# A two-layer decoder on one core: the softmax peak of two of four score banks applied by ScalarE's bias instead of a VectorE subtraction

## The chip, the core and the metric

The kernel runs on one core of a Trainium2 chip. The core's engines run side by side and meet only at semaphores: TensorE (PE; its weight loads are PEld), VectorE (DVE), ScalarE (ACT), GpSimd (POOL) and SyncE (SP, which here only issues DMAs). Each engine takes its own instructions strictly in program order. PSUM, into which TensorE writes, has eight banks of 128 partitions by 512 f32; SBUF is the working memory. The metric is the device time of one launch in microseconds (us), where less is better.

## What is computed

Two decoder layers on x of 16 x 128 x 256 (16 sequences, here called tiles, of 128 tokens). Every step is a sublayer, a residual sum and a layer norm:

```python
x = _layernorm(x + _L0_attn_ref(...))     # l0: latent attention with rotary embedding, 16 heads
x = _layernorm(x + _L0_xattn_ref(ctx, x)) # x0: linear attention
x = _layernorm(x + _L0_ffn_ref(...))      # f0: gated FFN, fp4 levels
x = _layernorm(x + _L1_attn_ref(...))     # l1: causal attention plus a second branch (ma)
x = _layernorm(x + _L1_xattn_ref(x, ctx)) # x1: cross attention and a ReLU FFN
x = _layernorm(x + _L1_ffn_ref(...))      # f1: one linear layer, fp6 levels
```

Three of these have a softmax over 128 keys, for 16 heads of each tile: l0, l1 and x1, thus 48 softmaxes of 128 x (16 heads x 128 keys). With the scale s, what is computed is exp(s * score - s * peak), with peak the largest score of a row and head; the sum of a row is taken along with the values and divided out later.

## The kernel before

**Staging.** Each tile goes through 55 stages (`STAGES`), and four tiles are under way at a time. `TIMELINE` is a table of numbers: it gives each stage of each tile a slot, with a tile 122 slots after the one before, and every engine writes its instructions for the stages in the order of these slots. No scheduler reorders anything: an instruction that waits holds back all that stands behind it on its engine. In the middle of the run the same pattern returns once per tile, with stages of four tiles laced into each other. Per tile it has one `l0_scores`, one `x1_scores` and one `l1_scores`, and in the pattern they come in this order; x1 and l1 stand close together.

**Banks.** Banks 0 to 3 (`s0` to `s3`) hold scores; banks 4 to 7 go round in a ring among all other results of TensorE. Two semaphores of a bank, full and empty, count its fills and its emptyings. `free` makes TensorE wait until the bank's last content has been read, `emptied` marks the instruction that has read it.

**A softmax.** TensorE writes the scores of 16 heads, 4 per bank, with the mask summed in. The banks are handled in the order `BANK_ORDER = (2, 3, 0, 1)`:

- VectorE (`softmax`, L912 to L939) takes the peak of 4 heads of a bank in one reduction (L918). For banks 2 and 3 it then writes the peak times -s to `low` (L925, 128 x 4). For banks 0 and 1 it subtracts the peak from the scores, 128 x 512, from PSUM into `prob` (L929), which also frees the score bank.
- ScalarE (`exps`, L649 to L666) takes exp of banks 2 and 3 head by head: 8 instructions of 128 x 128 that read PSUM, with a column of `low` as bias (L663). For banks 0 and 1 it takes exp of 128 x 512 at once, in place in `prob`, without a bias (L657).
- TensorE (`mix`, L1299 to L1309) turns `prob` over, 4 transposes per bank into a bank of the ring (recorded at L1240), ScalarE copies each into `probT` (recorded at L601), and TensorE weighs the values with it.

**What stands around it.** Helpers record much of the work under one line: all matmuls under L1125, transposes of tiles under L1240, copies by ScalarE under L601. Behind the exps of x1 on ScalarE stand the copy of the turned f1 input (L601), two biased reads of l1's queries (L712) and two tanh (L717), of which the last frees the bank that TensorE's third turn of x1's `prob` needs. Behind the exps of l1 stands the copy of the turned x of x0 (`xt_`, L601), which TensorE needs for `x0_project`. Behind the exps of l0 stand two copies of the turned FFN hidden (`scratch`, L601), each of which frees a ring bank, and then the first copy to `probT`, which frees a third; the matmuls of `f0_down` (with `w_dn`) need all three.

Of the kernel before, what the change touches and what calls it, by code (L numbers as in the profile page):

```python
# [14 lines left out]
P = 128  # L15
TILES, D, HEADS, HD, LAT = 16, 256, 16, 16, 32
FFN, HID = 704, 1024
KD = D // P
GROUP = 4
# [5 lines left out]
ALU = mybir.AluOpType  # L25
ACT = mybir.ActivationFunctionType
# [10 lines left out]
SCALES = {"l0": LAT ** -0.5, "l1": HD ** -0.5, "x1": HD ** -0.5}  # L37
# [38 lines left out]
S_BANKS = ["s0", "s1", "s2", "s3"]  # L76


BANK_ORDER = (2, 3, 0, 1)
# [19 lines left out]
SCORES = ["l0_scores", "l1_scores", "x1_scores"]  # L99
# [46 lines left out]
def of_turn(i, b, value):  # L146


    if isinstance(i, int):
        return value(i * GROUP + b)  # L150
    reg, off = i
    found = [value((turn + off) * GROUP + b) for turn in range(1, ITERS)]
    step = found[1] - found[0]
    assert all(found[n] == found[0] + n * step for n in range(len(found))), (b, found)
    return reg * step + (found[0] - step)


def at(i, stages, stage, b, n=1, j=0):


    seq = [(s, t) for _, s, t in TIMELINE if s in stages]
    return of_turn(i, b, lambda t: seq.index((stage, t)) * n + j + 1)


def decoder_kernel(nc, x, xT, ctxT, mask, cols, rows, const, bconst, c_attn, blocks, wqk, cproj,
                   x0_w, gate_up, down, l1_w, x1_w, w1, w2, fw, out):
    with ExitStack() as ctx:
        def sb(name, shape, dt=F32):
            return ctx.enter_context(nc.sbuf_tensor(name, shape, dt))

        def sem(name):
            return ctx.enter_context(nc.semaphore(name))

        bank = [ctx.enter_context(nc.psum_tensor(f"bank{k}", [P, 512], F32)) for k in range(8)]
# [65 lines left out]
        prob = sb("prob", [P, 4, 512])  # L240
# [1 line left out]
        ma_ = sb("ma_", [P, 4, 512])  # L242

        peak = sb("peak", [P, GROUP, HEADS])
        low = sb("low", [P, GROUP, 8])
        inv_sum = sb("inv_sum", [P, GROUP, HEADS])
        stats = sb("stats", [P, GROUP, 6])
        mean_var = sb("mean_var", [P, GROUP, 2])
# [35 lines left out]
        def long(ap, n):  # L284

            return ap.unsqueeze(2).broadcast_to([ap.shape[0], ap.shape[1], n])

        def rows4(ap):
            return ap.rearrange("p (c t) -> p c t", c=4)
# [35 lines left out]
        x_biased = sem("x_biased")  # L325
        q_swap, q_cos, q_sin, q_done = sem("q_swap"), sem("q_cos"), sem("q_sin"), sem("q_done")
        k_cos, k_swap, k_done = sem("k_cos"), sem("k_swap"), sem("k_done")
        peaked, lowered, exped, inverse = sem("peaked"), sem("lowered"), sem("exped"), sem("inverse")
        parted, varied, eps_in, rooted = sem("parted"), sem("varied"), sem("eps_in"), sem("rooted")
        x_new, affine = sem("x_new"), sem("affine")  # L330
        scaling, quant, dequant = sem("scaling"), sem("quant"), sem("dequant")
# [3 lines left out]
        def count(i, key):  # L335

            if i is None:
                return WHERE[key][0], WHERE[key][1] + 1
            stage, b, name = key
            return WHERE[stage, b, name][0], of_turn(i, b, lambda t: WHERE[stage, t, name][1] + 1)  # L340

        def wait_full(eng, i, key):

            k, value = count(i, key)
            eng.wait_ge(full[k], value)
            return bank[k]

        def wait_empty(eng, i, key):

            k, value = count(i, key)  # L350
            eng.wait_ge(empty[k], value)
# [7 lines left out]
        def emptied(ins, key):  # L359
            ins.then_inc(empty[WHERE[key][0]], 1)  # L360
# [236 lines left out]
        def _(act):  # L597
# [51 lines left out]
            def exps(layer):  # L649

                stage = layer + "_scores"

                def f(i, b):
                    for r in BANK_ORDER:
                        if r < 2:
                            wait_empty(act, i, (stage, b, S_BANKS[r]))
                            act.activation(prob[:, r, :], prob[:, r, :], ACT.Exp, scale=SCALES[layer])\  # L657
                                .then_inc(exped, 1)
                            continue
                        act.wait_ge(lowered, at(i, SCORES, stage, b, 2, r - 2))  # L660
                        for c in range(4):
                            h = 4 * (r - 2) + c
                            ins = act.activation(prob[:, r, c * P:(c + 1) * P], bank[r][:, c * P:(c + 1) * P],  # L663
                                                 ACT.Exp, scale=SCALES[layer], bias=low[:, b, h:h + 1])
                        emptied(ins, (stage, b, S_BANKS[r]))
                return f  # L666
# [93 lines left out]
        def _(dve):  # L760
# [10 lines left out]
            src = wait_full(dve, None, "p_g")  # L771
# [4 lines left out]
            src = wait_full(dve, None, "p_latb")  # L776
# [135 lines left out]
            def softmax(layer):  # L912

                stage = layer + "_scores"

                def top(i, b, r):
                    src = wait_full(dve, i, (stage, b, S_BANKS[r]))
                    dve.tensor_reduce(peak[:, b, 4 * r:4 * r + 4], rows4(src[:, :]), AX_X, ALU.max)\  # L918
                        .then_inc(peaked, 1)

                def take(i, b, r, n):
                    dve.wait_ge(peaked, at(i, SCORES, stage, b, 4, n))
                    if r >= 2:

                        dve.tensor_scalar(low[:, b, 4 * r - 8:4 * r - 4], peak[:, b, 4 * r:4 * r + 4],  # L925
                                          -SCALES[layer], None, ALU.mult).then_inc(lowered, 1)
                        return
                    src = bank[r]
                    emptied(dve.tensor_tensor(rows4(prob[:, r, :]), rows4(src[:, :]),  # L929
                                              long(peak[:, b, 4 * r:4 * r + 4], P), ALU.subtract),  # L930
                            (stage, b, S_BANKS[r]))

                def f(i, b):
                    for n, r in enumerate(BANK_ORDER):
                        top(i, b, r)
                        if n:
                            take(i, b, BANK_ORDER[n - 1], n - 1)
                    take(i, b, BANK_ORDER[3], 3)
                return f  # L939
# [167 lines left out]
        def _(pe):  # L1107
# [129 lines left out]
            def turn_tile(i, key, src, n=KD, moved=()):  # L1237
                dst = free(i, key, moved)
                for k in range(n):
                    ins = pe.transpose(dst[:, k * P:(k + 1) * P], src[:, k * P:(k + 1) * P], ident)  # L1240
                filled(ins, key)
# [57 lines left out]
            def mix(layer):  # L1299

                def f(i, b):
                    for r in BANK_ORDER:
                        key = (layer + "_mix", b, f"t{r}")
                        if r < 2:
                            pe.wait_ge(exped, at(i, SCORES, layer + "_scores", b, 2, r))
                        else:
                            wait_empty(pe, i, (layer + "_scores", b, S_BANKS[r]))
                        turn_tile(i, key, prob[:, r, :], 4)
                return f  # L1309

# [267 lines left out]
```

## Time and profile before

| | |
|---|---|
| median of 3 runs | 1174.74 us (1174.51 to 1176.31) |
| the profiled execution, its own time | 1172.23 us |
| its span, first to last instruction | 1170.4 us |
| mean granted clock of TensorE | 0.936 of full |
| PE busy | 946.8 us, 81% |
| DVE busy | 888.7 us, 76% |
| ACT busy | 509.1 us, 43% |
| POOL busy | 309.4 us, 26% |
| the chain that ended last | DVE 47%, PE 30%, ACT 11%, issue 6%, POOL 6% |

Shares of busy time say how much an engine does, not whether the end waits for it. The chain that ended last is followed back from the last instruction, at each step to what released it; its shares say where the end is set. The pattern of one tile takes about 65 us, and it is in its rows, in order of time, that one sees which engine is last at which point.

### The profile page before, as it was taken

How to read it: one execution, taken by the hardware profiler on the slowest of the kernel's cores; microseconds unless marked ns; L12 is line 12 of the kernel's file. 1: busy time of each engine (PE TensorE's matmuls, PEld its weight loads, DVE VectorE, ACT ScalarE, POOL GpSimd, SP SyncE). 2: the span in 40 equal slices, each digit the busy share in tenths (PEclk: the TensorE clock that was granted, in tenths of full speed). 3: DMA queues.
4: the chain of work that ended last, by engine and by line, in shares of the span. 5: the costliest groups of instructions: out<-in, count | busy, mean ns of one | idle time of the engine just before them, and what ended most of it. 6: DMA issues, size and time to landing. Idle time of an engine off the chain costs nothing.

```text
span 1170.4 us, 23205 instructions
## 1 busy us (share of the span) xinstructions
PE 946.8 (81%) x8774; PEld 752.5 (64%) x8774; DVE 888.7 (76%) x2135; ACT 509.1 (43%) x1377; POOL 309.4 (26%) x508
## 2 busy tenths in 40 slices
PE   5657778888888888888888888888888888878754
PEld 5444656676676776776767766767666767657633
DVE  3775677888797888788797888878887888777452
ACT  2322436363536355363636354453636263534320
POOL 2561121312222222223222232232222222312121
PEclk9677999999999999999999999999999999989876
DMA  9102000000000000000000000000000000000000
GB/s 338 37 5 73 10 8 15 3 19 8 20 8 15 10 17 10 14 14 3 20 7 15 13 15 11 16 11 3 24 3 20 3 6 8 6 6 6 6 4 5
DMA packets 24414, 24.47 MB, mean 21 GB/s; under 512 B 2305, under 2 KB 22641, under 8 KB 24177
## 3 DMA queue, kind: packets, MB, share of 16 engines
q1 hardware_dynamic: 24304, 22.98, 6.1%
q8 instruction: 72, 1.18, 0.4%
q14 instruction: 38, 0.30, 0.1%
HBM read 18.80 MB, written 2.10 MB: 18 GB/s over the span
## 4 chain that ended last, share of the span: by engine, by line
DVE 47%; PE 30%; ACT 11%; issue 6%; POOL 6%; DMA 0%; DVEq 0%; POOLq 0%; SPq 0%
PE bank L1125 21%; PE bank L1240 9%; DVE peak L918 7%; ACT prob L663 6%; ACT prob L657 3%; DVE ma_ L1037 3%; DVE stats L847 2%; DVE q_top L809 2%; DVE y_ L861 2%; POOL scratch L528 2%; POOL rstd L522 2%; DVE k_ L1061 2%; DVE scratch L905 2%; DVE x_ L873 1%; DVE k_ L1070 1%
## 5 line engine op out<-in xcount | busy, mean ns | idle before, releaser
L663 ACT ACTIVATE prob<-bank,low 128x128 f32<-128x128 f32 x384 | 104.4, 382 | 156.6 <-DVE low L925 156.6
L1240 PE MATMUL bank<-cst,prob 128*128 128x128 f32 x768 | 117.2, 303 | 54.7 <-DVE y_ L861 39.0
L519 POOL TENSOR_TENSOR var_eps<-mean_var,rsq 128x1 f32<-128x1 f32 x144 | 28.4, 198 | 468.3 <-DVE mean_var L850 468.3
L1240 PEld LDWEIGHTS bank<-cst,prob 128*128 128x128 f32 x768 | 96.1, 156 | 71.9 <-issue 62.6
L918 DVE TENSOR_REDUCE peak<-bank 128x4 f32<-128x512 f32 x192 | 126.3, 684 | 20.8 <-PE bank L1125 20.8
L601 ACT ACTIVATE xt_<-bank 128x256 f32<-128x256 f32 x144 | 54.9, 393 | 130.5 <-PE bank L1240 130.3
L601 ACT ACTIVATE probT<-bank 128x512 f32<-128x512 f32 x192 | 103.5, 602 | 17.4 <-PE bank L1240 17.4
L522 POOL TENSOR_TENSOR rstd<-var_eps,rsq 128x1 f32<-128x1 f32 x144 | 79.8, 554 | 11.3
L1125 PE MATMUL bank<-w_gu,xt_ 128*128 128x352 f32 x256 | 81.0, 470 | 1.5 <-ACT w_f L601 1.0
L1125 PE MATMUL bank<-xt_,w 128*128 128x128 f32 x512 | 70.5, 304 | 0.5 <-ACT xt_ L601 0.5
L1125 PEld LDWEIGHTS bank<-xt_,w 128*128 128x128 f32 x512 | 69.4, 221 | 1.2 <-ACT xt_ L601 1.2
L1125 PEld LDWEIGHTS bank<-w_gu,xt_ 128*128 128x128 f32 x256 | 49.9, 196 | 27.6 <-issue 3.2
L847 DVE BATCH_NORM_STATS2 stats<-y_ 128x6 f32<-128x256 f32 x144 | 61.5, 427 | 5.0
L1240 PE MATMUL bank<-cst,y_ 128*128 128x128 f32 x128 | 27.8, 300 | 45.7 <-DVE y_ L886 34.1
L563 POOL TENSOR_TENSOR scratch<-scratch,q_scale 128x704 f32<-128x704 f32 x16 | 22.2, 1385 | 156.7 <-DVE scratch L822 156.7
L1125 PE MATMUL bank<-k_,q_ 32*128 32x128 f32 (+2 forms) x1040 | 61.3, 347 | 0.0
L929 DVE TENSOR_TENSOR prob<-bank,peak 128x512 f32<-128x512 f32 x96 | 61.3, 679 | 0.0
L509 POOL TENSOR_TENSOR xb_<-x_,rowt 128x256 f32<-128x256 f32 x80 | 60.0, 757 | 2.7 <-DVE x_ L873 2.7
L657 ACT ACTIVATE prob<-prob 128x512 f32<-128x512 f32 x96 | 57.4, 676 | 0.0
L563 POOL TENSOR_TENSOR k_<-q_,q_scale 128x256 f32<-128x256 f32 x32 | 19.8, 617 | 137.4 <-DVE q_ L822 137.4
L1240 PE MATMUL bank<-cst,k_ 128*128 128x128 f32 x64 | 15.0, 319 | 50.5 <-POOL k_ L563 50.5
L638 ACT ACTIVATE scratch<-bank,lat_bias 128x128 f32<-128x128 f32 x128 | 36.5, 367 | 43.8 <-PE bank L1125 43.8
(180 smaller groups left out, 2202.7 us busy)
## 6 DMA issues: line engine op xcount, KB each, us to landing
xtin<-in_xT SPq DMA_DIRECT2D x16, 128.0 KB, 2.3
next_<-in_x SPq DMA_DIRECT2D x16, 128.0 KB, 6.9
ct_<-in_ctxT SPq DMA_DIRECT2D x16, 128.0 KB, 7.7
w<-in_w SPq DMA_DIRECT2D x2, 1024.0 KB, 6.1
out<-x_ SPq DMA_DIRECT2D x16, 128.0 KB, 1.7
next_<-x_ SPq DMA_DIRECT2D x16, 127.0 KB
rowt<-in_rows SPq DMA_DIRECT2D x1, 1664.0 KB, 7.7
w<-in_gate_up SPq DMA_DIRECT2D x2, 512.0 KB, 9.4
```

Of the source, the lines that this page charges most:

```text
L509: pool.tensor_tensor(xb_[:, b, :], source(b), term, ALU.add).then_inc(x_biased, 1)
L522: pool.tensor_tensor(rstd[:, b:b + 1], var_eps[:, b:b + 1], rsq[:, 1:2], ALU.pow)\
L563: pool.tensor_tensor(to(b).rearrange("p (a k) -> p a k", k=block), lev(b).rearrange("p (a k) -> p a k", k=block), long(q_scale[:, b % 2, a ...
L601: emptied(act.activation(dst, src, ACT.Copy), key)
L638: ins = act.activation(dst[:, c * P:(c + 1) * P], src[:, c * P:(c + 1) * P], ACT.Identity, bias=lat_bias[:, off + c:off + c + 1])
L657: act.activation(prob[:, r, :], prob[:, r, :], ACT.Exp, scale=SCALES[layer])\
L663: ins = act.activation(prob[:, r, c * P:(c + 1) * P], bank[r][:, c * P:(c + 1) * P], ACT.Exp, scale=SCALES[layer], bias=low[:, b, h:h + 1])
L847: dve.bn_stats(stats[:, b, :], y_[:, b, :]).then_inc(parted, 1)
L918: dve.tensor_reduce(peak[:, b, 4 * r:4 * r + 4], rows4(src[:, :]), AX_X, ALU.max)\
L929: emptied(dve.tensor_tensor(rows4(prob[:, r, :]), rows4(src[:, :]), long(peak[:, b, 4 * r:4 * r + 4], P), ALU.subtract), (stage, b, S_BANK ...
L1125: return pe.matmul(dst, lhsT, rhs, start=first, stop=last, **more)
L1240: ins = pe.transpose(dst[:, k * P:(k + 1) * P], src[:, k * P:(k + 1) * P], ident)
```

## The change

For banks 0 and 1, VectorE now does what it did for banks 2 and 3: it writes the peak times -s to `low`, and no longer subtracts. ScalarE takes exp of these banks too head by head from PSUM, with `low` as bias. `low` grows from 8 to 16 columns. Banks 0 and 1 are now freed by the fourth exp of each and no longer by the subtraction, and TensorE's turns wait for that instead of for the semaphore `exped`, which is gone. Per softmax 2 subtractions of 128 x 512 and 2 exps of 128 x 512 go; 2 products of 128 x 4 and 8 exps of 128 x 128 come.

```diff
-        low = sb("low", [P, GROUP, 8])
+        low = sb("low", [P, GROUP, HEADS])
...
-                    for r in BANK_ORDER:
-                        if r < 2:
-                            wait_empty(act, i, (stage, b, S_BANKS[r]))
-                            act.activation(prob[:, r, :], prob[:, r, :], ACT.Exp, scale=SCALES[layer])\
-                                .then_inc(exped, 1)
-                            continue
-                        act.wait_ge(lowered, at(i, SCORES, stage, b, 2, r - 2))
+                    for n, r in enumerate(BANK_ORDER):
+                        act.wait_ge(lowered, at(i, SCORES, stage, b, 4, n))
                         for c in range(4):
-                            h = 4 * (r - 2) + c
+                            h = 4 * r + c
                             ins = act.activation(prob[:, r, c * P:(c + 1) * P], bank[r][:, c * P:(c + 1) * P],
                                                  ACT.Exp, scale=SCALES[layer], bias=low[:, b, h:h + 1])
                         emptied(ins, (stage, b, S_BANKS[r]))
...
                     dve.wait_ge(peaked, at(i, SCORES, stage, b, 4, n))
-                    if r >= 2:
-
-                        dve.tensor_scalar(low[:, b, 4 * r - 8:4 * r - 4], peak[:, b, 4 * r:4 * r + 4],
-                                          -SCALES[layer], None, ALU.mult).then_inc(lowered, 1)
-                        return
-                    src = bank[r]
-                    emptied(dve.tensor_tensor(rows4(prob[:, r, :]), rows4(src[:, :]),
-                                              long(peak[:, b, 4 * r:4 * r + 4], P), ALU.subtract),
-                            (stage, b, S_BANKS[r]))
+                    dve.tensor_scalar(low[:, b, 4 * r:4 * r + 4], peak[:, b, 4 * r:4 * r + 4],
+                                      -SCALES[layer], None, ALU.mult).then_inc(lowered, 1)
...
-                        if r < 2:
-                            pe.wait_ge(exped, at(i, SCORES, layer + "_scores", b, 2, r))
-                        else:
-                            wait_empty(pe, i, (layer + "_scores", b, S_BANKS[r]))
+                        wait_empty(pe, i, (layer + "_scores", b, S_BANKS[r]))
```

No other instruction changes its place. On ScalarE, from the exps of x1 to what follows the exps of l1, there stood:

```order
L663 ACTIVATE prob<-bank,low 128x128 x8
L657 ACTIVATE prob<-prob 128x512 x2
L601 ACTIVATE xt_<-bank 128x256
L712 ACTIVATE q_<-bank,colt 128x128 x2
L717 ACTIVATE xt_<-bank,k_bias 128x128 x2
L723 ACTIVATE ka_<-xt_,colt 128x256 x2
L601 ACTIVATE probT<-bank 128x512 x4
L663 ACTIVATE prob<-bank,low 128x128 x8
L657 ACTIVATE prob<-prob 128x512 x2
L601 ACTIVATE xt_<-bank 128x256
L601 ACTIVATE yt_<-bank 128x512
```

and after the exps of x1 there now stands, to the same point (L658 is the exp of every bank, L707, L712 and L718 are L712, L717 and L723 of before):

```order
L707 ACTIVATE q_<-bank,colt 128x128 x2
L712 ACTIVATE xt_<-bank,k_bias 128x128 x2
L718 ACTIVATE ka_<-xt_,colt 128x256 x2
L601 ACTIVATE probT<-bank 128x512 x4
L658 ACTIVATE prob<-bank,low 128x128 x16
L601 ACTIVATE xt_<-bank 128x256
L601 ACTIVATE yt_<-bank 128x512
```

Where 8 narrow and 2 wide exps stood there are 16 narrow ones, and the same copies stand behind them.

## Rows read from the trace of the kernel before

**Rows 1.** The page: PE's and others' busy time; the chain by engine and line.

```profile
PE 946.8 (81%) x8774; PEld 752.5 (64%) x8774; DVE 888.7 (76%) x2135; ACT 509.1 (43%) x1377; POOL 309.4 (26%) x508
...
DVE 47%; PE 30%; ACT 11%; issue 6%; POOL 6%; DMA 0%; DVEq 0%; POOLq 0%; SPq 0%
PE bank L1125 21%; PE bank L1240 9%; DVE peak L918 7%; ACT prob L663 6%; ACT prob L657 3%; DVE ma_ L1037 3%; DVE stats L847 2%; DVE q_top L809 2%; DVE y_ L861 2%; POOL scratch L528 2%; POOL rstd L522 2%; DVE k_ L1061 2%; DVE scratch L905 2%; DVE x_ L873 1%; DVE k_ L1070 1%
```

**Rows 2.** Groups of the softmax: count | busy us, mean ns | idle before.

```profile
L663 ACT ACTIVATE prob<-bank,low 128x128 f32<-128x128 f32 x384 | 104.4, 382 | 156.6 <-DVE low L925 156.6
...
L929 DVE TENSOR_TENSOR prob<-bank,peak 128x512 f32<-128x512 f32 x96 | 61.3, 679 | 0.0
...
L657 ACT ACTIVATE prob<-prob 128x512 f32<-128x512 f32 x96 | 57.4, 676 | 0.0
...
L925 DVE TENSOR_SCALAR low<-peak 128x4 f32<-128x4 f32 x96 | 22.0, 229 | 0.0
```

**Rows 3.** The chain in order of time, x1 then l1: start us, us, what.

```profile
565.86 1.04 ACT prob L657 x2
...
567.68 0.53 ACT xt_ L717 x2
...
574.52 1.04 ACT prob L657 x2
...
575.88 1.60 PE bank L1125 x12
```

**Rows 4.** Timeline at x1's exps: start us, us, engine, line, what [idle before <-releaser].

```profile
563.68 2.17 ACT L663 ACTIVATE prob<-bank,low 128x128 f32<-128x128 f32 x8 [3.25 <-DVE low L925]
565.70 1.20 ACT L657 ACTIVATE prob<-prob 128x512 f32<-128x512 f32 x2
566.73 0.43 ACT L601 ACTIVATE xt_<-bank 128x256 f32<-128x256 f32 x1
...
568.34 1.06 PE L1240 MATMUL bank<-cst,prob 128*128 128x128 f32 x8 [0.40 <-ACT xt_ L717]
```

**Rows 5.** Timeline at l1's exps, DVE, then PE.

```profile
573.49 1.28 DVE L929 TENSOR_TENSOR prob<-bank,peak 128x512 f32<-128x512 f32 x2
574.69 0.68 DVE L967 TENSOR_TENSOR scratch<-bank,rowt 128x512 f32<-128x512 f32 x1
...
575.88 1.16 PE L1125 MATMUL bank<-xt_,w_x 128*128 128x128 f32 x8 [1.08 <-ACT xt_ L601]
```

**Rows 6.** Timeline at l0's exps of a tile with full clock: ACT, then PE.

```profile
678.76 0.92 ACT L601 ACTIVATE scratch<-bank 128x512 f32<-128x512 f32 x2
679.50 0.66 ACT L601 ACTIVATE probT<-bank 128x512 f32<-128x512 f32 x1
...
681.08 2.95 PE L1125 MATMUL bank<-w_dn,scratch 128*128 128x256 f32 x12
```

**Rows 7.** Timeline at l0's exps of an earlier tile: PE.

```profile
547.37 0.63 PE L1240 MATMUL bank<-cst,prob 128*128 128x128 f32 x4 [1.82 <-DVE y_ L861]
548.50 2.79 PE L1240 MATMUL bank<-cst,prob 128*128 128x128 f32 x12 [0.51 <-DVE y_ L861]
```

**Rows 8.** Busy time by stretch, one tile's pattern each; PEclk is the granted clock.

```profile
546.48:611.34 64.86, 55.91 (x542) 44.79 (x542) 53.09 (x131) 31.21 (x86) 17.15 (x30) 0.97 0.04 12
...
870.71:937.05 66.34, 57.64 (x542) 46.42 (x542) 53.26 (x131) 31.20 (x86) 17.16 (x30) 0.95 0.04 10
937.05:1000.25 63.20, 54.24 (x542) 43.25 (x542) 53.08 (x131) 31.00 (x86) 17.11 (x30) 1.00 0.02 7
```

**Rows 9.** The same view, four short stretches at half clock.

```profile
275.43:278.85 3.42, 3.42 (x19) 3.42 (x17) 3.14 (x7) 0.69 (x1) 0.00 (x0) 0.50 0.00 0
548.50:551.92 3.42, 3.42 (x14) 3.26 (x15) 1.76 (x5) 2.21 (x4) 1.92 (x4) 0.50 0.00 0
664.55:667.97 3.42, 3.42 (x18) 3.42 (x17) 3.14 (x7) 0.69 (x1) 0.00 (x0) 0.50 0.00 0
1002.47:1005.89 3.42, 3.42 (x15) 3.23 (x14) 1.72 (x6) 2.02 (x4) 1.72 (x4) 0.50 0.00 0
```

More of the change, by code:

```diff
@@ L327, in decoder_kernel @@
         k_cos, k_swap, k_done = sem("k_cos"), sem("k_swap"), sem("k_done")
-        peaked, lowered, exped, inverse = sem("peaked"), sem("lowered"), sem("exped"), sem("inverse")
+        peaked, lowered, inverse = sem("peaked"), sem("lowered"), sem("inverse")
         parted, varied, eps_in, rooted = sem("parted"), sem("varied"), sem("eps_in"), sem("rooted")
```

## Prediction, made from the kernel before alone

> **What bounds the kernel now.** I read the page first, then the chain in order of time, then the timeline where the chain touches a softmax, then the granted clock by stretch.
>
> The page makes VectorE look like the engine to relieve: it is 76% busy, with 47% of the chain, and ScalarE is 43% busy with 11% of it [rows 1]. But the chain by line names the exps too: L663 has 6% and L657 has 3%, while L929, the subtraction that the change takes away, is not among the lines shown [rows 1]. 3% of 1170.4 us is about 34 us, and a pair of the wide exps takes 1.04 us on the chain [rows 3]; 34 / 1.04 is about 32 pairs. There are 48 softmaxes, 16 each of l0, x1 and l1. So two of three softmaxes have their exps on the path.
>
> The chain in order of time says which [rows 3]. At x1 it runs through the wide exps, the tanh of l1_project (L717) and then TensorE's turns; at l1 it runs through the wide exps and straight on to a matmul. The timeline gives the reason. At x1, 8 turns on TensorE waited 0.40 us for ScalarE's L717, which had to free a ring bank [rows 4]. At l1, the matmuls of x0_project waited 1.08 us for the copy of xt_, which stands behind the exps on ScalarE [rows 5]. At l0 it is otherwise: TensorE waits for VectorE's residual sum (L861) twice, 1.82 and 0.51 us [rows 7].
>
> TensorE's clock is the second matter. Three tiles' patterns have the same number of instructions and take 63.20 us at clock 1.00, 64.86 at 0.97 and 66.34 at 0.95 [rows 8]. The difference is stretches at half clock (1.2 GHz instead of 2.4), none, one or two of them per pattern. Rows 9 has four: 12 of them begin between 275 and 1003 us (the first and the last row are the first and the last of these), about one per tile. The one at l0's turns (548.50) comes after TensorE had idled 1.82 us and shortly after that 0.51 us [rows 7]; the other (664.55) comes after a gap in which TensorE waits for VectorE's affine norm of x1. One of them costs 64.86 - 63.20 = 1.66 us, and two cost 3.14.
>
> **The change part by part.**
>
> *ScalarE, each softmax.* 8 narrow exps pace at 565.70 - 563.68 = 2.02 us, 0.253 each. The two wide ones pace at 566.73 - 565.70 = 1.03 us [rows 4]. The change puts 8 more narrow ones where the two wide ones stood: + 2.02 - 1.03 = + 0.99 us until the next instruction on ScalarE starts. The added exps are of the very form of L663 (128 x 128 from PSUM, a column of `low`), so the row is the price itself; bounds are the smallest step between two (0.25) and the full 0.382 us that one takes alone [rows 2], which would give + 1.0 to + 2.0 us; I take 0.253, since they are issued back to back.
>
> The Trainium skill has another price. Its page "ScalarE: Activation LUTs" (What ACT_TABLE_LOAD costs) puts an ACTIVATE with a pointer bias at about 280 ns plus 0.833 ns per column, one with immediates at 186 ns plus the same, with 93 ns of overlap. As an estimate from that page 8 narrow exps would take 2.35 us and the two wide ones 1.04 us, + 1.31 per softmax. The wide pair agrees with the trace's 1.03 us and the narrow ones are quicker in the trace (2.02), so the measurement decides; by the page the sum below would be 10 us higher. The page also speaks against the change in principle: the fixed part is paid once per instruction.
>
> *VectorE, each softmax.* Two subtractions go, which pace at 574.69 - 573.49 = 1.20 us [rows 5]. Two products to `low` come; those there are average 0.229 us [rows 2], but part of each lies under the reduction beside it, and the last of the four has to wait for its own peak as the last subtraction did. I put the saving at 0.9 us (bounds 0.7 and 1.1), 43 us over 48 softmaxes. What of it reaches the end is the question, not its size.
>
> *x1, 16 times.* All four `low` are written before ScalarE gets to bank 0, so ScalarE runs through 16 exps and reaches the copy, L712 and L717 0.99 us later. TensorE's turns of bank 0 already waited 0.40 us for L717, so there is no slack: the wait grows to about 1.4 us, l1's scores come 0.99 later, and with them VectorE's next peaks. VectorE has its 0.9 us in hand, but it waits there for TensorE. 16 x 0.99 = 15.8 us.
>
> *l1, 16 times.* The copy of xt_ comes 0.99 us later, and TensorE already waited 1.08 us for it. VectorE is idle after this until x0's results come, so its saving is again spent in waiting. 16 x 0.99 = 15.8 us.
>
> *l0, 16 times.* Here VectorE's residual sum comes 0.9 us earlier and TensorE could begin its turns earlier. But the third and fourth turns need ring banks that ScalarE frees by the two copies to `scratch`, and f0_down needs the bank that the first copy to `probT` frees; these three stand behind the exps. Before, with full clock, that copy began at 679.50 and took 0.66, so it ended at 680.16, and f0_down began at 681.08 [rows 6]. The three copies move back by 0.99: the copy ends at 681.15, and f0_down can begin at about 681.2. ScalarE's loss eats VectorE's gain to within 0.1 us: + 0.1 x 16 = + 1.6 us. The bounds are - 0.3 (where the turns run at half clock, ScalarE's copies had more slack) and + 0.3, so - 5 to + 5 us.
>
> *Bank release.* Score banks 0 and 1 are freed about 2 us later than before. The next scores are written over 3 us after the turns that need the same exps, in TensorE's own order, so nobody waits: 0. The product to `low` queues nothing new, and `exped` costs nothing to drop. SP and GpSimd are untouched.
>
> *TensorE's clock.* The added 0.99 us at l1 makes one gap of about 2.1 us where there was one of 1.08, and at x1 about 1.4 where there was 0.40. The gap of 1.82 us at l0 is cut in two, but the one before the third turn grows. Gaps of this size are what stood before half-clock stretches so far [rows 7, 9]. So the pattern now has one more place at which a stretch can follow, at l1, where TensorE is on the path right after. Bounds: none of today's 12 stretches left (- 20 us), to one more in each of the 13 patterns in full swing (+ 21 us). I take an extra one in every other pattern: 6 x 1.66 = + 10 us, because one place goes weaker (l0) and one is new.
>
> **The sum.** The profiled execution took 1172.2 us, its span plus 1.8. 1172.2 + 15.8 + 15.8 + 1.6 + 10 = 1215.4 us. The median of the runs lies 2.5 us above the profiled execution, so 1218 us.
>
> **Rivals.**
>
> *The exps cost what they cost and the clock does as before.* 1174.7 + 31.6 + 1.6 = 1208 us. For it: today's number of stretches hardly varies from tile to tile. Against: longer gaps on TensorE.
>
> *The new rhythm spares the stretches.* Patterns without any exist today, 63.20 us [rows 8], and a different length of the pattern may miss them all: 1208 - 20 = 1188 us. In between lie 1190 to 1205.
>
> *More stretches or dearer exps.* One more stretch in each pattern, 1208 + 21 = 1229 us; or exps nearer to 0.29 us each, 10 us more, 1228 with the forecast's clock.
>
> *Faster.* VectorE with its 47% of the chain decides, at l0: if TensorE's f0_down doesn't need to wait for ScalarE's copies, the 0.9 us comes through 16 times, and if in x1 and l1 the copies behind the exps were hidden, nothing would be lost: 1174.7 - 14 = 1160 us. It decides only if both waits on ScalarE in rows 4 and 5 are misread, that is, if TensorE would have been held there by something else for another 0.99 us. The rows name ScalarE with 0.40 and 1.08 us of plain idle time, and the chain passes there. For no change at all the l0 gain would have to come through in double.
>
> That the change doesn't do what it says can be left out: the built kernel has 16 narrow exps per softmax on ScalarE and no subtraction on VectorE.
>
> **How the numbers follow.** Forecast with about half an extra stretch per pattern (1210 to 1224): 0.45. Clock as before (1204 to 1210): 0.22. Fewer stretches (1188 to 1204): 0.12. More stretches or dearer exps (1224 to 1238): 0.17. Faster: 0.03. No change: 0.01. Range 1198 to 1230: it leaves out half of the cases with fewer stretches, a third of those with more, and the rivals below. A measurement of this kernel can tell about 0.2% (2.3 us) from no change; slower by more than that has 0.96, faster 0.03, within it 0.01.
>
> **What would show it.** On the page: ACT's busy time up by some 45 us and its share of the chain up from 11% to 14 or 15%, DVE's busy time down by 45 to 55. In the timeline at l1: the wait of x0_project for the copy of xt_ at about 2.1 us, and at x1 the turns' wait for the tanh at about 1.4. At l0: TensorE's wait before the third turn naming ScalarE's copy to scratch instead of VectorE's sum. A pattern with full clock takes about 65.2 us, and those with stretches 66.9 and 68.5. The prediction is wrong if that pattern stays at 63.2 (then the path isn't through these exps), or if the number of half-clock stretches is far from 18.

## The result, and the profile after

The changed kernel takes 1270.01 us (median of 4 runs, 1268.87 to 1274.74), beside 1175.53 us for the kernel before in the same job: 1.081 times as long, 95% interval 1.078 to 1.0841. The forecast was 1218, with a range up to 1230. Slower was right; the loss is 95 us where 43 were forecast.

From the page of the changed kernel, the lines that answer [rows 1] (busy time, the chain by engine and by line), and the groups that answer [rows 2] (count | busy us, mean ns | idle before):

```profile
span 1267.1 us, 23493 instructions
PE 1002.9 (79%) x8774; PEld 793.8 (63%) x8774; DVE 837.1 (66%) x2135; ACT 558.0 (44%) x1665; POOL 307.0 (24%) x508
...
DVE 38%; PE 33%; ACT 19%; POOL 5%; issue 4%; DMA 0%; DVEq 0%; POOLq 0%; SPq 0%
PE bank L1113 23%; ACT prob L658 16%; PE bank L1228 10%; DVE peak L913 5%; DVE ma_ L1025 2%; DVE stats L842 2%; POOL scratch L528 2%; POOL rstd L522 2%; DVE q_top L804 2%; DVE k_ L1049 1%; DVE scratch L900 1%; DVE x_ L868 1%; DVE k_ L1058 1%; DVE y_ L881 1%; DVE y_ L878 1%
...
L658 ACT ACTIVATE prob<-bank,low 128x128 f32<-128x128 f32 x768 | 203.5, 413 | 173.4 <-DVE low L918 173.4
```

```profile
L918 DVE TENSOR_SCALAR low<-peak 128x4 f32<-128x4 f32 x192 | 36.9, 204 | 0.1
```

The work moved as meant. VectorE is busy 51.6 us less (888.7 to 837.1), ScalarE 48.9 us more (509.1 to 558.0). TensorE has the same 8774 matmuls, yet is busy 56.1 us more (946.8 to 1002.9). That is the first sign of a slower clock. ScalarE has 19% of the chain, where the prediction looked for 14 or 15%. The 16% of L658 are about 203 us, which is 48 times the 4.23 us that 16 exps take; so now all three softmaxes have their exps on the chain, l0's too.

The same view of stretches as in [rows 8], of three patterns of the changed kernel, from one start of l0's exps to the next (us, then busy us with counts of PE, PEld, DVE, ACT, POOL, then PEclk):

```profile
660.49:732.22 71.73, 60.58 (x544) 48.17 (x543) 49.79 (x131) 34.17 (x103) 16.95 (x30) 0.90 0.04 12
732.22:803.86 71.64, 60.47 (x544) 48.16 (x543) 49.71 (x131) 34.17 (x104) 16.97 (x30) 0.90 0.04 11
874.48:943.19 68.71, 57.18 (x542) 45.83 (x542) 49.79 (x131) 34.13 (x103) 16.96 (x30) 0.95 0.04 12
```

A pattern takes 71.7 us where it took 63.2 to 66.3 [rows 8], at a clock of 0.90. The next rows, of the same view, are the stretches at half clock within one pattern and the first of the next one; they answer [rows 9]:

```profile
647.98:651.39 3.41, 3.37 (x10) 2.23 (x11) 3.20 (x7) 1.07 (x2) 0.73 (x1) 0.50 0.02 5
665.04:668.45 3.41, 3.09 (x12) 2.85 (x13) 1.58 (x4) 2.61 (x6) 1.34 (x4) 0.50 0.00 0
685.52:688.93 3.41, 3.30 (x32) 2.49 (x36) 0.75 (x2) 3.02 (x6) 0.00 (x0) 0.50 0.02 5
695.76:699.17 3.41, 3.41 (x16) 3.41 (x17) 0.55 (x2) 0.99 (x3) 0.10 (x1) 0.50 0.00 0
719.66:723.07 3.41, 3.28 (x10) 2.14 (x11) 3.23 (x8) 1.07 (x2) 0.73 (x1) 0.50 0.00 0
```

There are four per pattern: at the turn of x1's hidden, at l0's turns, at x1's turns and behind l1's exps. The kernel before had one per pattern, taking one with another. Counted by the granted clock in the traces, over twelve patterns in the middle of the run (222.0 to 998.2 us before, 230.3 to 1087.1 us after), it had 11, and the changed kernel has 45. The fifth row is the first one again, 71.68 us later. The pattern returns with its stretches in the same places, tile after tile: from 217.90 to 839.12 us every pattern has its four. One pattern that has only two of them (874.48) takes 3.0 us less than its neighbours, 1.5 for each.

The gaps that TensorE has in these places, from the timeline of the changed kernel (start us, us, engine, line, what [idle before <-releaser]); the first two rows are l0, then come x1 and l1, then the turn of the hidden:

```profile
663.54 0.63 PE L1228 MATMUL bank<-cst,prob 128*128 128x128 f32 x4 [0.50 <-DVE y_ L856]
665.36 1.94 PE L1228 MATMUL bank<-cst,prob 128*128 128x128 f32 x8 [1.20 <-ACT scratch L601]
...
684.60 0.63 PE L1228 MATMUL bank<-cst,prob 128*128 128x128 f32 x4 [1.66 <-ACT xt_ L601]
...
685.63 1.94 PE L1228 MATMUL bank<-cst,prob 128*128 128x128 f32 x8 [0.40 <-ACT xt_ L712]
...
695.69 2.04 PE L1113 MATMUL bank<-xt_,w_x 128*128 128x128 f32 x8 [2.11 <-ACT xt_ L601]
...
648.02 0.69 PE L1228 MATMUL bank<-cst,y_ 128*128 128x128 f32 x2 [2.21 <-DVE y_ L881]
```

The gap ahead of the turn of the hidden is no longer than it was in the kernel before, where it also stood in patterns that had no stretch behind it, as here:

```profile
598.25 0.44 PE L1240 MATMUL bank<-cst,y_ 128*128 128x128 f32 x2 [2.21 <-DVE y_ L886]
```

### The profile page after: what moved, and what is told of

Its sections match the earlier page's. It is cut to its first block, busy times and chain, and to the rows that moved or that the text cites. A ratio compares the mean times of both kernels' runs of the same rounds, so it can differ in the third digit from the quotient of the medians.

```text
span 1267.1 us, 23493 instructions
## 1 busy us (share of the span) xinstructions
PE 1002.9 (79%) x8774; PEld 793.8 (63%) x8774; DVE 837.1 (66%) x2135; ACT 558.0 (44%) x1665; POOL 307.0 (24%) x508
## 4 chain that ended last, share of the span: by engine, by line
DVE 38%; PE 33%; ACT 19%; POOL 5%; issue 4%; DMA 0%; DVEq 0%; POOLq 0%; SPq 0%
PE bank L1113 23%; ACT prob L658 16%; PE bank L1228 10%; DVE peak L913 5%; DVE ma_ L1025 2%; DVE stats L842 2%; POOL scratch L528 2%; POOL rstd L522 2%; DVE q_top L804 2%; DVE k_ L1049 1%; DVE scratch L900 1%; DVE x_ L868 1%; DVE k_ L1058 1%; DVE y_ L881 1%; DVE y_ L878 1%
## 5 line engine op out<-in xcount | busy, mean ns | idle before, releaser
L658 ACT ACTIVATE prob<-bank,low 128x128 f32<-128x128 f32 x768 | 203.5, 413 | 173.4 <-DVE low L918 173.4
L1228 PE MATMUL bank<-cst,prob 128*128 128x128 f32 x768 | 138.8, 336 | 78.6 <-ACT xt_ L601 24.1
L1228 PEld LDWEIGHTS bank<-cst,prob 128*128 128x128 f32 x768 | 113.9, 177 | 97.1 <-issue 72.5
L1113 PE MATMUL bank<-xt_,w_x 128*128 128x128 f32 x256 | 46.8, 342 | 34.4 <-ACT xt_ L601 34.4
L856 DVE TENSOR_TENSOR y_<-bank,x_ 128x256 f32<-128x256 f32 x32 | 13.6, 425 | 80.6 <-PE bank L1113 80.6
L1113 PEld LDWEIGHTS bank<-xt_,w_x 128*128 128x128 f32 x256 | 41.5, 245 | 40.1 <-ACT xt_ L601 38.9
L1113 PE MATMUL bank<-k_,q_ 32*128 32x128 f32 (+2 forms) x1040 | 66.2, 366 | 0.0
L1113 PE MATMUL bank<-xt_,w 128*128 128x128 f32 x512 | 64.8, 288 | 0.5 <-ACT xt_ L601 0.5
L1113 PEld LDWEIGHTS bank<-k_,q_ 32*128 32x128 f32 (+1 forms) x1040 | 49.8, 209 | 13.4 <-issue 10.0
L1113 PE MATMUL bank<-w_dn,scratch 128*128 128x256 f32 x192 | 56.0, 442 | 0.8 <-ACT scratch L601 0.8
```

The costliest lines, as they stand in the source:

```text
L1113: return pe.matmul(dst, lhsT, rhs, start=first, stop=last, **more)
```

## The experiments

Two theories. **A, the clock:** of the 6.8 us that a pattern gained (64.86 to 71.7), some 2 are ScalarE's longer exps on the path, and the rest is half clock behind TensorE's longer gaps. **B, the price:** the exps themselves cost over 3 us at x1 and at l1, and the clock only goes along. All runs of one job share their runs of the kernel before (1173.6 to 1175.3 us).

### TensorE kept busy in its gaps

In both kernels TensorE gets fillers, matmuls whose result is overwritten unread. The diff is that of the changed kernel, 35 fillers per tile. The kernel before has other gaps and gets 7 ahead of l0's first turn and 2 behind it, 1 behind x1's second turn, 4 ahead of x0_project and 9 ahead of the turn of the hidden, 23 in all:

```diff
+            def keep_busy(n, dst):
+                for _ in range(n):
+                    mm(dst[:, :], ident_bf, bcst[:, P:P + 512], skip_group_check=True)
...
                         wait_empty(pe, i, (layer + "_scores", b, S_BANKS[r]))
+                        if r == 2:
+                            keep_busy({'l0': 2}.get(layer, 0), bank[2])
                         turn_tile(i, key, prob[:, r, :], 4)
+                        keep_busy({('l0', 2): 2, ('l0', 3): 5, ('x1', 2): 7, ('x1', 3): 1}.get((layer, r), 0), bank[2])
...
+                for _, t in scores_before("x0_project", i, b):
+                    wait_empty(pe, t // GROUP, ("l1_scores", t % GROUP, "s2"))
+                    keep_busy(9, bank[2])
                 dst = free(i, ("x0_project", b, "q"), [("x0_turn_x", b, "xt")])
...
+                keep_busy(9, free(i, ("x1_turn_h", b, "xt")))
                 pe.wait_ge(affine, at(i, AFFINES, "x1_affine1", b, 2, 1))
```

> The changed kernel with fillers on TensorE: matmuls of 128x512 bf16 whose result is overwritten before anyone reads it, put into its gaps (behind the turns of banks 2 and 3 of x1's and l0's prob, ahead of x0_project, ahead of x1's turn of the hidden). Theory A (the clock): of the 6.8 us that a tile's pattern has gained, 2.0 are ScalarE's longer exps at x1 and l1 and 4.8 are three more half-clock stretches; with the gaps filled the clock stays at 1.00, a pattern takes about 65.2 us and the whole about 1187 us. Theory B (the price): the exps themselves cost over 3 us at x1 and l1 each and the clock only goes along; then the clock rises and the time stays within 15 us of 1270.

> The kernel before with fillers of the same kind, as many as its shorter gaps take. Theory A: its 12 half-clock stretches in the middle go, 12 x 1.66 = 20 us, about 1155 us; the distance to the changed kernel with fillers is then 32 us, ScalarE's part alone. Theory B: about 1175 us, since the fillers add nothing but work, and the distance between the two stays near 95 us.

Measured: the changed kernel with fillers takes 1189.24 us, the kernel before with fillers 1152.66 (ratio 0.9814, 0.9791 to 0.9837). So both are as theory A has them, and B falls: the changed kernel gets back 81 us without one exp being touched. The kernel before gets back 22 us too, so the distance between the two shrinks from 95 to 36.6 us. One pattern of each, the changed kernel's first, in the view of stretches:

```profile
486.94:552.58 65.64, 62.23 (x578) 46.29 (x578) 49.60 (x131) 33.95 (x104) 16.97 (x30) 1.00 0.04 12
```

```profile
538.97:602.15 63.18, 59.56 (x566) 45.21 (x566) 53.05 (x131) 30.99 (x86) 17.12 (x30) 1.00 0.05 13
```

Both have full clock, and differ by 2.46 us. The timeline tells where, by the starts of the exps of l0, x1 and l1. With fillers, the changed kernel:

```profile
552.58 4.23 ACT L673 ACTIVATE prob<-bank,low 128x128 f32<-128x128 f32 x16 [5.14 <-DVE low L935]
570.52 4.23 ACT L673 ACTIVATE prob<-bank,low 128x128 f32<-128x128 f32 x16 [3.25 <-DVE low L935]
580.21 4.23 ACT L673 ACTIVATE prob<-bank,low 128x128 f32<-128x128 f32 x16 [1.09 <-DVE low L935]
```

and the kernel before:

```profile
538.97 2.17 ACT L673 ACTIVATE prob<-bank,low 128x128 f32<-128x128 f32 x8 [5.14 <-DVE low L935]
...
556.51 2.17 ACT L673 ACTIVATE prob<-bank,low 128x128 f32<-128x128 f32 x8 [3.24 <-DVE low L935]
...
565.17 2.17 ACT L673 ACTIVATE prob<-bank,low 128x128 f32<-128x128 f32 x8 [1.09 <-DVE low L935]
```

From l0 to x1 it is 17.94 us against 17.54, from x1 to l1 9.69 against 8.66, and the rest of the pattern 38.01 against 36.98. So l0 costs 0.40 us, x1 1.03 and l1 1.03. These are the prices of the change at full clock. Over 16 tiles they come to 39 us; the two kernels with fillers differ by 36.6. The remaining 58 of the 95 us go when the gaps are filled and the clock is back: they are the clock's price.

The kernel before with fillers is the fastest version of all: 22 us (1.9%) faster than the kernel as it was. This is TensorE doing more work (23 fillers per tile; 59.56 us busy in a pattern where it was 54.24 at full clock [rows 8]) and ending earlier.

### One half of the change at a time

VectorE's half: the subtractions go, but ScalarE takes the wide exps as before, now straight from PSUM. The peaks of banks 0 and 1 are left out of these exps, so this kernel does not compute the same softmax; it has VectorE's work of the changed kernel and ScalarE's number of instructions of the kernel before.

```diff
...
+                        if r < 2:
+                            ins = act.activation(prob[:, r, :], bank[r][:, :], ACT.Exp, scale=SCALES[layer])
+                        else:
...
```

> VectorE's part alone: the subtractions go, as in the change, but ScalarE takes exp of banks 0 and 1 at once, 128x512, from PSUM and without the peak (the peak of these heads is left out, so that the work on ScalarE stays as many instructions as before). Theory A: VectorE's 0.9 us are waited away at x1 and l1 and worth up to 0.8 at l0, where ScalarE's copies are no later than before: 1160 us, between 1150 and 1175 with the clock's stretches falling otherwise. A rival, that freeing score banks 0 and 1 later (by ScalarE) is what hurts: near 1200 or above.

Measured: 1153.19 us (ratio 0.9818, 0.9793 to 0.9842), as theory A has it and a little better. Releasing score banks 0 and 1 from ScalarE hurts nothing. At l0, f0_down begins 4.68 us after the exps instead of 5.38 (675.70 to 681.08, the latter in [rows 6]): 0.7 us per tile, 11 us in all. With that go 6 stretches at half clock in the twelve middle patterns where there were 11, some 8 us more. The start of the exps in the kernel before, and then the timeline of this run, ACT and PE:

```profile
675.70 2.17 ACT L663 ACTIVATE prob<-bank,low 128x128 f32<-128x128 f32 x8 [4.90 <-DVE low L925]
```

```profile
539.59 2.17 ACT L676 ACTIVATE prob<-bank,low 128x128 f32<-128x128 f32 x8 [5.14 <-DVE low L938]
541.60 1.13 ACT L672 ACTIVATE prob<-bank 128x512 f32<-128x512 f32 x2
...
544.27 2.95 PE L1138 MATMUL bank<-w_dn,scratch 128*128 128x256 f32 x12
```

So VectorE's relief is worth something, at one of three places, as long as ScalarE isn't later.

ScalarE's half: VectorE subtracts as before, and the exp of banks 0 and 1 is cut in four.

```diff
-                            act.activation(prob[:, r, :], prob[:, r, :], ACT.Exp, scale=SCALES[layer])\
-                                .then_inc(exped, 1)
+                            for c in range(4):
+                                ins = act.activation(prob[:, r, c * P:(c + 1) * P], prob[:, r, c * P:(c + 1) * P],
+                                                     ACT.Exp, scale=SCALES[layer])
+                            ins.then_inc(exped, 1)
```

> ScalarE's part alone: VectorE subtracts as before, and ScalarE takes exp of banks 0 and 1 in four pieces of 128x128, in place in prob and without a bias. Theory A: 1.0 us more at x1, l1 and now at l0 too (3 x 16 us = 48), and more stretches at half clock: 1250 to 1300 us. A rival, that reading PSUM by 8 more exps with a bias is what is dear: near 1200 us.

Measured: 1207.11 us (ratio 1.028). The expectation was wrong by over 40 us, in two terms. The pieces without a bias, read from SBUF, pace faster than those with one:

```profile
583.83 1.74 ACT L669 ACTIVATE prob<-prob 128x128 f32<-128x128 f32 x8
585.42 0.42 ACT L611 ACTIVATE xt_<-bank 128x256 f32<-128x256 f32 x1
```

8 take 1.59 us here, and 2.02 in [rows 4]; cutting costs 0.56 us per softmax, not 0.99. And at l0 nothing was lost: f0_down begins 5.37 us after the exps, as before.

```profile
564.27 2.17 ACT L678 ACTIVATE prob<-bank,low 128x128 f32<-128x128 f32 x8 [4.90 <-DVE low L940]
...
569.64 2.95 PE L1140 MATMUL bank<-w_dn,scratch 128*128 128x256 f32 x12
```

The 0.56 at x1 and l1 make 18 us; the other 14 go with the clock, 0.919 against 0.936, with 18 stretches in the middle where there were 11. The rival that the expectation named (near 1200 us) came nearer than theory A, and has a part of the truth: of the 0.99 us, 0.43 are what 8 narrow exps cost more from PSUM and with a bias than from SBUF and without one. Neither half has those 8 exps, and the halves (22 us less and 32 us more) don't add up to the whole (95 us more).

### One softmax at a time, and half of each

Here `NEW` lists the layers and banks that go the new way, all others go as before:

```diff
-                        if r < 2:
+                        if r < 2 and (layer, r) not in NEW:
```

> The change in l0's softmax alone; x1 and l1 as before. By the working of the prediction ScalarE's copies eat VectorE's gain: 1175 us plus 1.6, and the clock's stretches decide the rest, 1165 to 1185 us. If l0 has its share of the 95 us, it gives about 1205.

> The change in x1's softmax alone. ScalarE's step of 1.0 us per tile gives 1191 us with the clock as before. Theory A (the clock) says that TensorE's gaps at x1 grow (second turn waits for the copy, third for the tanh), so that further stretches appear: 1191 to 1225, and that the three parts don't add up to the whole, since it takes the length of the whole pattern for the stretches to fall at each place. If the parts simply add up, x1 and l1 give about 1222 each.

> The change in l1's softmax alone: 1191 us with the clock as before; with a stretch behind the 2.1 us gap ahead of x0_project in every pattern 1212. Adding up of parts would give about 1222.

> Half of the change in all three softmaxes: bank 1 the new way, bank 0 as before. ScalarE's step is 0.5 us at x1 and at l1: 16 us, 1191 with the clock as before. If the time grew with the work it would be 1222, half of 95 us more. Theory A expects anything between 1171 (stretches gone) and 1210, not on the line between the two kernels.

Measured: l0 alone 1193.18 us (ratio 1.0161, 1.0138 to 1.0184), x1 alone 1205.73, l1 alone 1207.84, one bank of each 1203.93 (1.025, 1.0224 to 1.0276).

x1 alone and one bank of each lie in the ranges of theory A, l1 alone between its 1191 and its 1212 us. The expectation for l0 alone failed: it costs 19.6 us, at a clock of 0.921 and with 17 stretches in the middle instead of 11. Its exps weren't on the chain before; with the change they are, but at 0.40 us per tile that is only 6 us. A copy of this variant with fillers separates the two:

> The change in l0's softmax alone, with all gaps filled. l0 alone was 19.6 us slower than before although its exps are not on the path. Theory A: that was the clock; with fillers 1153 us as the kernel before with fillers, plus 0.1 to 0.4 us per tile for ScalarE's later copies, 1154 to 1160. If l0 is dear by itself, 1170 or more. It is also the test whether VectorE's relief is worth anything where it can count: below 1150 it would be.

It takes 1157.23 us, 4.6 more than the kernel before with fillers (in another job, with its kernel before within 0.4 us of that one's). So l0's change costs about 5 us by itself, and 15 by the clock. It is also no gain: where VectorE's relief could count, ScalarE's later copies take it back.

The parts add up to 19.6 + 32 + 34 = 86 of the 95 us, which is closer than I had thought; that parts don't add is only weakly borne out. One bank of each gives 30 us, where half of the whole would be 47: doubling the change tripled the cost. The stretches in the middle go from 11 to 17 with one bank and to 45 with two.

### One gap filled at a time

The changed kernel, with the fillers in one place only:

> The changed kernel with fillers in one gap only, the 2.1 us ahead of x0_project behind l1's exps. Theory A: of the four half-clock stretches of a pattern at least the one behind this gap goes, 13 x 1.6 = 21 us, 1249 us, and a shorter pattern may lose others too: 1210 to 1250. If the clock followed TensorE's share of busy time over the whole pattern, one gap filled of four would do nothing or everything.

> The same with fillers only in the gaps at x1 (1.7 us behind the turn of bank 2, 0.4 behind that of bank 3). Theory A as above: 1210 to 1250 us.

> The same with fillers only in the gap of 2.2 us ahead of the turn of x1's hidden, which the change has not lengthened. Theory A: the gap precedes a stretch in the changed kernel in every pattern, in the one before only in some; filling it takes that stretch away: 1210 to 1250 us. If only gaps that the change made matter, near 1270.

Measured, all three in the range of theory A: 1224.14 us with the gap behind l1's exps filled, 1240.39 with those at x1, 1229.32 with the one ahead of the turn of the hidden. So each gap by itself is worth 30 to 46 us, more than one stretch in each of 13 patterns at 1.5 to 1.66 us each (20 to 22 us). Together, and with l0's gaps, which were not filled alone, they give back 81, not their sum of 116. The gap ahead of the hidden's turn is no longer than before, and filling it is worth 41 us all the same.

The traces show that the stretches depend on each other. Of the 45 in the twelve middle patterns there are left 16 with l1's gap filled, 26 with x1's and 18 with the hidden's: filling one place in twelve patterns took away 19 to 29, so stretches at the other places went too. It may be the length of the pattern that couples them; this was not tried by itself, and by what rule they fall where they do is not settled here.

### The account

TensorE's time at half clock is 2 x (1 - clock) x span, with the clock and the span of the profiled execution. A stretch is counted as 3.41 us at half clock (one of double length as two):

| kernel | median us | span us | clock | at half clock, us | stretches in the twelve middle patterns |
|---|---|---|---|---|---|
| before | 1174.74 | 1170.4 | 0.936 | 150 | 11 |
| after | 1270.01 | 1267.1 | 0.89 | 279 | 45 |
| after, gaps filled | 1189.24 | 1187.1 | 0.964 | 85 | 0 |
| before, gaps filled | 1152.66 | 1151.4 | 0.959 | 94 | 0 |
| VectorE's half | 1153.19 | 1152.5 | 0.939 | 141 | 6 |
| ScalarE's half | 1207.11 | 1205.7 | 0.919 | 195 | 18 |
| l0 alone | 1193.18 | 1191.4 | 0.921 | 188 | 17 |
| x1 alone | 1205.73 | 1200.2 | 0.926 | 178 | 18 |
| l1 alone | 1207.84 | 1205.6 | 0.917 | 200 | 18 |
| one bank of each | 1203.93 | 1202.4 | 0.919 | 195 | 17 |
| after, l1's gap filled | 1224.14 | 1220.7 | 0.93 | 171 | 16 |
| after, x1's gaps filled | 1240.39 | 1242.4 | 0.912 | 219 | 26 |
| after, hidden's gap filled | 1229.32 | 1229.2 | 0.926 | 182 | 18 |
| l0 alone, gaps filled | 1157.23 | 1158.1 | 0.96 | 93 | 0 |

Changed kernel against the kernel before: 129 us more at half clock, of which half is lost, 65 us, and 2 x 1.03 + 0.40 = 2.46 us per tile, 39 us. That is 104 for the 97 us by which the spans differ. With l0 alone it is 19 + 6 for 21 us, with x1 alone 14 + 16 for 30. For l1 alone (25 + 16 for 35) and for one bank of each (22 + 16 for 32) it is 6 us too much. With all gaps filled it promises 9 to 10 us more gain than there is (the changed kernel: 39 - 32 = 7, measured 17). So not all time at half clock costs its full price. The traces say where it doesn't: at the two ends of the run. In the kernel before some 115 us at half clock lie outside the twelve middle patterns, and the fillers bring them to 97; by the rule that would be 9 us, but the ends get only 2 us shorter (394.2 to 392.3). In the middle the account closes: with fillers the kernel before needs 17.1 us less (776.2 to 759.1) for 11 stretches of 1.66 us, 18 us. The changed kernel needs 80.7 us more (856.9) for 34 stretches more at 1.5 to 1.66 us and 12 x 2.46 us, 81 to 86 us.

## Why the prediction was wrong, point by point

- **Which softmaxes are on the path: right for the kernel before.** x1 and l1 carry the exps serially, 1.03 us each at full clock where 0.99 was worked out from [rows 4]. The wait of x0_project is 2.11 us, as forecast, and names the copy behind the exps. In place of the 31.6 us of the sum stand 33. The count of 32 pairs by which the prediction began was coarser than it looked: 3% of 1170.4 us is 35 us, and a share in whole per cent allows 28 to 39 pairs. The chain in order of time is what carries this step.
- **l0: right in mechanism, small in size.** TensorE's third turn waits 1.20 us for ScalarE's copy to `scratch`, as forecast. It costs 0.40 us per tile, 6 us and not 1.6, and lies beyond the upper bound of 0.3: I let f0_down follow the copy to `probT`, but the third and fourth turns, 0.9 us in all, come after the copy to `scratch` and end later still. The changed kernel with fillers, ACT and then PE (the exps began at 552.58):

```profile
556.58 0.98 ACT L611 ACTIVATE scratch<-bank 128x512 f32<-128x512 f32 x2
...
557.44 1.07 PE L1250 MATMUL bank<-cst,prob 128*128 128x128 f32 x8
558.34 2.95 PE L1135 MATMUL bank<-w_dn,scratch 128*128 128x256 f32 x12
```

The prediction didn't see what follows from this: l0's exps come onto the path, where VectorE's sum had been. The chain of the changed kernel in order of time:

```profile
660.49 4.23 ACT prob L658 x16
664.73 0.49 ACT scratch L601
...
665.36 1.94 PE bank L1228 x8
```

- **x1's gaps: wrong.** I had named the copy of the f1 input among what stands behind x1's exps, but not followed whose bank it frees: that of TensorE's *second* turn. So the added time stands ahead of the second turn (1.66 us) and the third still waits 0.40 for the tanh, not 1.4. On the path this is the same 1.03 us; for the clock it is a gap of 1.66 us between 0.6 us of work, and then a stretch.
- **The clock: this is the step that failed.** The sum had 10 us, 6 stretches more in the whole run, and its upper bound one more per pattern, 21 us. There are three more per pattern, 34 in the twelve middle ones, and the clock costs 58 us; the prediction's own sign of being wrong, a number of stretches far from 18, has come true. The mechanism was named (longer gaps, half clock behind them), and the sum even said that the pattern had one more place for it. The bound was wrong because it counted places newly made. The gap ahead of the hidden's turn was there before and was followed by a stretch in some patterns only; now it is in nearly every one. In the kernel before four gaps could each have a stretch, and patterns had 0, 1 or 2 [rows 8]. By what is known now the upper bound was all of them in each pattern, 3 x 1.66 x 13 = 65 us more, and 1270 us would have been inside. Why the stretches fall at all four places in nearly every pattern stays open.
- **VectorE's saving: right, and worth nothing.** The page shows 51.6 us less busy time. Behind x1 and l1 it is waited away. The peaks of l1, which come behind x1's exps, waited 1.11 us for TensorE in a pattern before, and now wait 3.47 us (ScalarE's 1.03 us and TensorE's half clock are in this too). Before and after:

```profile
570.95 1.29 DVE L918 TENSOR_REDUCE peak<-bank 128x4 f32<-128x512 f32 x2 [1.11 <-PE bank L1125]
```

```profile
689.73 1.29 DVE L913 TENSOR_REDUCE peak<-bank 128x4 f32<-128x512 f32 x2 [3.47 <-PE bank L1113]
```

- **Freeing the score banks later at no cost: right**, as the run with VectorE's half alone shows.
- **The rival that the new rhythm spares the stretches** (1188 us) happened nowhere by itself; with fillers it is 1189.24.

## What to carry to other kernels

Before work is moved off the busiest engine, look at what stands behind it on the engine that takes it, in its strict order: 44% busy, and yet its exps are on the path at all three places. Where a kernel's TensorE is between full and half clock, a microsecond more of waiting has two prices, the wait and the clock behind it. Bound the second by every gap that could have a stretch, not by those that have one now; and if a few gaps of 1 to 2 us recur, fill them with matmuls whose results nobody reads, which here gave 22 us of 1175.

## What the runs showed of the hardware that I had not expected

- Half-clock stretches of 3.41 us each come with idle gaps of only 1 to 2.2 us (in the middle patterns of both kernels TensorE is never idle for more than 2.34 us), and a program with a repeating pattern can settle into having them in the same places each time: four per 71.68 us, from 217.90 to 839.12 us without exception.
- Fillers of 128x512 bf16 start 0.22 us apart (the first of the nine ahead of x0_project at 582.60, the fourth at 583.26) and hold the clock at 1.00 through every pattern of the middle. The last six of the nine, and the matmuls that they run up to, from the timeline of the changed kernel with fillers:

```profile
583.26 1.46 PE L1135 MATMUL bank<-bcst 128*128 128x512 bf16 x6
584.76 1.16 PE L1135 MATMUL bank<-xt_,w_x 128*128 128x128 f32 x8
```

- An exp of 128x128 paces at 0.20 us from SBUF without a bias and at 0.25 from PSUM with one. Of 128x512 without a bias, two take 1.20 us from SBUF [rows 4] and 1.13 from PSUM (in the run with VectorE's half). That speaks for the bias and against PSUM as what makes the narrow ones dearer; a narrow exp from PSUM without a bias was not run.
